# A two-layer relational graph attention kernel: the first keys are asked for after the query spread instead of beside it

## The chip, the cores and the metric

The kernel runs on one core of one Trainium2 chip. The metric is the device time of the whole program in microseconds (us). Work is divided among TensorE (PE), VectorE (DVE), ScalarE (ACT), GpSimd (POOL) and SyncE (SP), each with its own instruction stream; they meet at semaphores only. Sixteen DMA engines move data between DRAM and the on-chip memory.

## The reference

A graph of 1250 nodes (768 features) and 20000 edges, each with a source, a target and one of three types. A graph convolution comes first, then two relational attention layers (4 heads, then 1 head). Of one attention layer, what matters here:

```python
xr = jnp.einsum('nd,rdf->rnf', x, W)      # rows of the three relations
oi = xr[etype, dst]; oj = xr[etype, src]
qi = oi @ q                               # query score of the edge's target
kj = oj @ k                               # key score of the edge's source
alpha = leaky_relu(qi + kj, 0.2)
m = segment_max(alpha, dst)
e = exp(alpha - m[dst]); z = segment_sum(e, dst)
a = e / (z[dst] + 1e-16)
out = segment_sum(a * oj, dst) + b
```

## The kernel before, in words

Edges are sorted by target into slots of 128. Ten tiles of 128 nodes own the slots; two slots make a pair. The first node tile has far more pairs than the others, since low node numbers are drawn as targets more often. In this data there are 83 pairs.

Each attention layer `l` (1, 2) begins with the scores. Both scores of a node are computed first, per relation, without the big projection. Then two things are brought to the edge slots:

- **The query score, on TensorE.** `spread(j, q16, ...)` multiplies one-hot matrices (`stT`) with the ten tiles of query values. It is a loop for each tile, with six pairs in each turn: 12 slots, 36 small matmuls in layer 1 (line 1172) and 12 in layer 2 (line 1169). Over the ten tiles there are 17 turns, 612 or 204 matmuls. `spread_close` (line 1177) ends it and raises `q_spread[l]`.
- **The key score, on GpSimd.** `kst` is written to DRAM (line 396, `s_keys`), and `ask_keys(n)` asks for batch `n` by 12 indirect DMAs, each of 128 rows of 4 floats (line 490). An ask waits until the one 4 before it (layer 1) or 2 before it (layer 2) has landed. They go in GpSimd's own order.

VectorE waits for `q_spread[l]` (line 907), forms `qs` (lines 911 to 921) and raises `qs_ready`. GpSimd, once it has asked for batches 0 and 1 and `qs_ready` is there, does `score(0)` (lines 500, 504, 508: sum, the negative part, `al`), asks for batch 2, does `score(1)`, asks for batch 3, and so on for 14 batches. VectorE follows with the running maxima of the pairs whose `al` is there (lines 944, 959, 964), and at the end of a node tile with `maxima` (line 934).

On TensorE, after the query spread and once `spread_read` says that VectorE has read the banks, comes `project`: 30 node tiles (3 relations of 10) of 24 matmuls each (line 1255). `MAX_AT` puts between them the steps of the maxima: after project 11 the transposes of maxima of tile 0 (line 1273), after 14 of tile 1, after 17 of tile 2 and the spread of maxima of tile 0, and so on; the last ones stand after project 29. For a transpose TensorE waits for VectorE (`z_in`, `z_read`). After all of it GpSimd gathers the projected rows (line 459) for the weighted sums, which begin when TensorE gives the ring free (line 1283).

The maxima's spread uses the same function `spread` and the same lines 1172 and 1169.

SP loads the weights of the second relation in layer 1 (line 380) once VectorE has ended `prepare`, and those of the third relation during the projections.

Of the kernel before, what the change touches and what calls it, by code (L numbers as in the profile page):

```python
# [92 lines left out]
def gnn_kernel(nc, x, src, dst, edge_type, W0, b0, W1, q1, k1, b1, W2, q2, k2, b2, out):  # L93
# [12 lines left out]
    with ExitStack() as ctx:  # L106
# [3 lines left out]
        def sem(name):  # L110
            return ctx.enter_context(nc.semaphore(name))
# [173 lines left out]
        q_spread = {l: sem(f"q_spread{l}") for l in (1, 2)}  # L285
# [28 lines left out]
        def load_bounds(eng):  # L314

            eng.wait_ge(bounds_ready, 1)
            return [0] + [eng.value_load(bounds[0:1, j:j + 1], min_val=j if j < NT else (E + PAIR - 1) // PAIR, max_val=MAXPAIRS) for j in range(1, NT + 1)]
# [107 lines left out]
        @block.gpsimd  # L425
        def _(pool):
            nc.gpsimd.iota(iota_f[:, :], [[1, T]], base=0, channel_multiplier=0, allow_small_or_imprecise_dtypes=True).then_inc(pool_c, 1)
            nc.gpsimd.iota(iota_h[:, :], [[1, T]], base=0, channel_multiplier=0, allow_small_or_imprecise_dtypes=True).then_inc(pool_c, 1)
            nc.gpsimd.iota(iota_p[:, :], [[0, 1]], base=0, channel_multiplier=1, allow_small_or_imprecise_dtypes=True).then_inc(pool_c, 1)
            nc.gpsimd.memset(half[:, :], -0.5).then_inc(pool_c, 1)  # L430
            nc.gpsimd.memset(zero16[:, :], 0.0).then_inc(pool_c, 1)
            nc.gpsimd.memset(ones[:, :], 1.0).then_inc(pool_c, 1)
            nc.gpsimd.memset(idxr[:, T:T + KB], 0).then_inc(pool_c, 1)
            pool.wait_ge(pool_c, 7)
            bnd = load_bounds(pool)
            pool.wait_ge(slots_f, 1)
            pool.sem_inc(turn, 1)

            def targets(first, end):
                for c in range(first * PB, end * PB):  # L440

                    pool.wait_ge(perm_free, c + PB + 1)
                    pool.sem_inc(turn, 1)
                    nc.gpsimd.tensor_scalar(oh_tg[:, c % PB, :], iota_h[0:EP, 0:P], dloc[:, c:c + 1], None, ALU.is_equal).then_inc(tg_in, 1)  # L444

            targets(0, 1)
            pool.wait_ge(var_ready, 1)
            nc.gpsimd.tensor_tensor(rstd[:, :], vare[:, :], half[:, :], ALU.pow).then_inc(rstd_ready, 1)
            targets(1, GROUPS)
            pool.wait_ge(deg_ready, 1)  # L450
            nc.gpsimd.tensor_tensor(dinv[:, :], deg[:, :], half[:, :], ALU.pow).then_inc(dinv_ready, 1)
            groups = (bnd[NT] + (RING - 1)) // RING
            rest = (bnd[NT] + (RING - 1 - RING * FIXED)) // RING

            def gather_rows(l, idx):

                for t in range(2 * RING * FIXED):
                    pool.wait_ge(w_used[l], t + 1)
                    nc.gpsimd.indirect_dma_start(ring[:, t % (2 * RING), 0:WIDTH[l]], None, rows[l], bass.IndirectOffsetOnAxis(idx[:, t:t + 1], 0)).then_inc(g_sem[l][t % (2 * RING)], 16)  # L459

                with pool.Fori(0, rest) as g:
                    for side in range(2):

                        pool.wait_ge(g_in[l], 2 * RING * g + (2 * RING * FIXED + RING * side + 1))
                        nc.gpsimd.tensor_copy(idxs[:, RING * side:RING * (side + 1)], idx[:, ds(g * (2 * RING) + (2 * RING * FIXED + RING * side), RING)]).then_inc(ix[l], 1)
                        pool.wait_ge(ix[l], 2 * g + (side + 1))
                        pool.sem_inc(turn, 1)
                        for s in range(RING * side, RING * (side + 1)):
                            if s % 2 == 0:

                                pool.wait_ge(w_used[l], g * (2 * RING) + (2 * RING * FIXED + s + 2))
                                pool.sem_inc(turn, 1)
                            nc.gpsimd.indirect_dma_start(ring[:, s, 0:WIDTH[l]], None, rows[l], bass.IndirectOffsetOnAxis(idxs[:, s:s + 1], 0)).then_inc(g_sem[l][s], 16)

            pool.wait_ge(slots_ready, 1)
            pool.wait_ge(s_rows0, 16 * (NT + 1))
            gather_rows(0, idx0)
            pool.wait_ge(var_ready, 2)
            nc.gpsimd.tensor_tensor(rstd[:, :], vare[:, :], half[:, :], ALU.pow).then_inc(rstd_ready, 1)
            for l in (1, 2):  # L480
                H = HEADS[l]

                flight = KFLIGHT[l]

                def ask_keys(n):

                    for t in range(n * KB, (n + 1) * KB):
                        if t >= flight:
                            pool.wait_ge(k_in[l][t % flight], 16 * (t // flight))
                        nc.gpsimd.indirect_dma_start(kb[:, n % KSEMS, t % KB, 0:4], None, keys[l], bass.IndirectOffsetOnAxis(idxr[:, t:t + 1], 0)).then_inc(k_in[l][t % flight], 16)  # L490

                def score(n, slot, lows, looped=False):

                    batch = al[:, ds(n * (KB * H), KB * H)]
                    for s in range(flight):
                        pool.wait_ge(k_in[l][s], n * (16 * KB // flight) + 16 * KB // flight)
                    if looped or n > 0:
                        pool.wait_ge(al_step[l], n * (KB // 2))
                    pool.sem_inc(turn, 1)
                    nc.gpsimd.tensor_tensor(summed[:, 0:KB * H].rearrange("p (c h) -> p c h", h=H), kb[:, slot, :, 0:H], qs[:, ds(n * (KB * H), KB * H)].rearrange("p (c h) -> p c h", h=H), ALU.add).then_inc(k_sum[l], 1)  # L500
                    pool.wait_ge(k_sum[l], n + 1)
                    if looped:
                        pool.sem_inc(turn, 1)
                    nc.gpsimd.tensor_scalar(low[:, 0:KB * H], summed[:, 0:KB * H], 0.0, SLOPE - 1.0, ALU.min, ALU.mult).then_inc(k_low[l], 1)
                    pool.wait_ge(k_low[l], lows)
                    if looped:
                        pool.sem_inc(turn, 1)
                    nc.gpsimd.tensor_tensor(batch, summed[:, 0:KB * H], low[:, 0:KB * H], ALU.add).then_inc(al_step[l], KB // 2)  # L508

                pool.wait_ge(g_in[l - 1], 2 * RING * groups + (RING + 1))  # L510
                pool.sem_inc(turn, 1)
                pool.wait_ge(s_keys, 16 * R * l)
                ask_keys(0)
                ask_keys(1)
                pool.wait_ge(qs_ready, l)
                for n in range(KSURE):
                    score(n, n % KSEMS, n + 1)
                    if n + 2 < KSURE:
                        ask_keys(n + 2)


                with pool.Fori(1, (bnd[NT] + (255 - (KSURE + 1) * (KB // 2))) // 256 + 2) as m:
                    n = m + (KSURE - 1)
                    nc.gpsimd.tensor_copy(idxk[:, :], idxr[:, ds(n * KB, KB)]).then_inc(k_low[l], 1)
                    pool.wait_ge(k_low[l], m * 2 + (KSURE - 1))
                    pool.sem_inc(turn, 1)
                    for k in range(KB):
                        pool.wait_ge(k_in[l][k % flight], n * (16 * KB // flight) + 16 * (k // flight))
                        pool.sem_inc(turn, 1)
                        nc.gpsimd.indirect_dma_start(kb[:, KSURE % KSEMS, k, 0:4], None, keys[l], bass.IndirectOffsetOnAxis(idxk[:, k:k + 1], 0)).then_inc(k_in[l][k % flight], 16)  # L530
                    score(n, KSURE % KSEMS, m * 2 + KSURE, True)
                for side in range(2):
                    pool.wait_ge(stage_out[l][side], 16 * R * NT // 2)
                pool.wait_ge(rows_go[l], 1)
                gather_rows(l, idxr)
# [791 lines left out]
```

## Time and profile before

| | |
|---|---|
| median of 3 runs | 1750.67 us (1749.24 to 1755.21) |
| the profiled execution's own time | 1749.11 us |
| its span | 1747.3 us |
| PE busy | 1504.7 us (86%), 6326 matmuls |
| POOL busy | 1019.1 us (58%) |
| DVE busy | 927.5 us (53%) |
| ACT busy | 220.0 us (13%) |
| POOL line 490 (asks for keys) | 312 of them, 331.3 us busy |

Busy time is a sum over stages that have different limits. What the change meets is read from the stages where it stands: in layer 1 from about 485 us to 865 us, in layer 2 from about 1155 us to 1482 us.

### The profile page before, as it was taken

Reading aid. Unit: us, or ns where it says so; the run is one execution under the profiler, and the core shown is the slowest. Engines: PE = TensorE matmul, PEld = TensorE weight load, DVE = VectorE, ACT = ScalarE, POOL = GpSimd, SP = SyncE. Lnnn points to the kernel's source line nnn. Section 1 sums busy time; section 2 is a strip of 40 time slices with the busy share of each in tenths; the row PEclk is TensorE's granted clock in tenths of the full one; section 3 lists DMA queues with packets and bytes.
Section 4 is the critical chain, followed back from the end, with each engine's and each line's share of the span. In section 5 each row is a group of like instructions: output and inputs, shape, how many; then the busy total and the mean of one; then the engine's idle time right before and its main releaser. Section 6 shows DMA issues by size and latency. Waiting matters only on the chain.

```text
span 1747.3 us, 25349 instructions
## 1 busy us (share of the span) xinstructions
PE 1504.7 (86%) x6326; PEld 879.1 (50%) x6330; DVE 927.5 (53%) x2169; ACT 220.0 (13%) x530; POOL 1019.1 (58%) x1112
## 2 busy tenths in 40 slices
PE   5989999889955998699799989955997998898986
PEld 2445554555544554466554445433554655454553
DVE  8576722333342888888677777603433345222232
ACT  1545200000000111011100023320110111000000
POOL 1598266664433778873167777515656662666664
PEclk9988999999975999789899999965998999999999
DMA  8201588888720222111288887630231111888888
GB/s 299 103 19 41 189 266 267 267 290 264 240 66 2 56 89 59 20 38 38 84 264 264 262 252 243 195 105 2 55 110 38 38 47 54 276 263 265 263 259 269
DMA packets 86808, 271.76 MB, mean 156 GB/s; under 512 B 32156, under 2 KB 32531, under 8 KB 86743
## 3 DMA queue, kind: packets, MB, share of 16 engines
q0 software_dynamic: 51072, 199.44, 37.8%
q1 hardware_dynamic: 34807, 65.62, 10.5%
q10 hardware_dynamic: 864, 5.90, 0.9%
q8 instruction: 34, 0.56, 0.1%
q14 instruction: 31, 0.25, 0.0%
HBM read 239.28 MB, written 31.62 MB: 155 GB/s over the span
## 4 chain that ended last, share of the span: by engine, by line
PE 67%; issue 12%; POOL 9%; DMA 6%; DVE 4%; ACT 1%; DVEq 1%; another core or an unknown queue 0%; POOLq 0%; SPq 0%; PEldq 0%; ACTq 0%
PE ps L1255 13%; PE ps L1295 12%; PE ps L1228 11%; POOL ring L490 6%; PE ps L1297 6%; PE ps L1298 6%; PE ps L1126 5%; DMA ring<-keys,idxr 4%; PE ps L1172 3%; PE ps L1169 2%; PE ps L1189 2%; PE ps L1076 2%; PE ps L1047 1%; PE ps L1089 1%; DMA ring<-rows,idxr 1%
## 5 line engine op out<-in xcount | busy, mean ns | idle before, releaser
L1255 PE MATMUL ps<-wreg,hT 128*128 128x384 f32 x1440 | 488.4, 502 | 7.3 <-PEq L1248 6.7
L490 POOL DMA_INDIRECT ring<-keys,idxr x312 | 331.3, 1062 | 193.6 <-issue 80.1
L459 POOL DMA_INDIRECT ring<-rows,idxr x304 | 311.1, 1024 | 220.8 <-PEq L1283 76.3
L1255 PEld LDWEIGHTS ps<-wreg,hT 128*128 128x128 f32 x1440 | 281.3, 197 | 203.1 <-issue 25.9
L1295 PE MATMUL ps<-ring,zw 128*128 x664 | 230.5, 500 | 26.1 <-DVE zw L1024 17.0
L1228 PE MATMUL ps<-ring,zw 128*128 x664 | 226.0, 497 | 24.0 <-DVE zw L853 12.5
L959 DVE TENSOR_TENSOR hn<-hn,al 128x1024 f32 (+1 forms) x166 | 137.5, 828 | 169.2 <-POOL al L508 107.5
L459 POOL DMA_INDIRECT ring<-rows,idx x152 | 145.9, 960 | 118.3 <-PE ps L1228 65.4
L1295 PEld LDWEIGHTS ps<-ring,zw 128*128 128x128 f32 x664 | 124.0, 192 | 126.5 <-issue 57.0
L1228 PEld LDWEIGHTS ps<-ring,zw 128*128 128x128 f32 x664 | 124.6, 192 | 119.9 <-issue 54.6
L1022 DVE TENSOR_TENSOR ring<-ring,al x166 | 159.3, 960 | 39.8 <-SPq L377 21.1
L1297 PE MATMUL ps<-ring,zw 128*128 x332 | 138.7, 500 | 29.8 <-DVE zw L1027 25.0
L1027 DVE TENSOR_SCALAR zw<-iota_f,tl,al 128x128 f32<-128x128 f32 x166 | 60.3, 368 | 181.8 <-PE ps L1298 116.1
L853 DVE TENSOR_SCALAR zw<-iota_f,tl,ring 128x128 f32<-128x128 f32 x166 | 58.4, 356 | 180.6 <-PE ps L1228 129.2
L444 POOL TENSOR_SCALAR stT<-iota_h,stT 125x128 f16<-125x128 f16 x160 | 106.5, 683 | 56.6 <-PE ps L1091 28.6
L964 DVE TENSOR_TENSOR zw<-zw,hn 128x1024 f32<-128x1024 f32 (+1 forms) x166 | 136.3, 821 | 0.1
L1298 PE MATMUL ps<-ring,zw 128*128 x332 | 135.2, 489 | 0.0
L1297 PEld LDWEIGHTS ps<-ring,zw 128*128 128x128 f32 x332 | 60.5, 191 | 81.5 <-issue 49.0
L1126 PE MATMUL ps<-ring,hT 128*128 128x384 f32 x240 | 88.0, 523 | 0.0
L1298 PEld LDWEIGHTS ps<-ring,zw 128*128 128x128 f32 x332 | 63.4, 191 | 44.3 <-issue 0.6
L944 DVE TENSOR_SCALAR hn<-iota_f,tl 128x128 f32 x332 | 82.4, 296 | 0.3 <-issue 0.3
L638 ACT ACTIVATE stage<-ps,rstd 128x384 f32<-128x384 f32 x60 | 34.9, 582 | 328.4 <-PE ps L1255 267.0
(185 smaller groups left out, 1231.4 us busy)
## 6 DMA issues: line engine op xcount, KB each, us to landing
wreg<-in_L_gnn_W SPq DMA_DIRECT2D x11, 2304.0 KB, 9.2
rows<-stage SPq DMA_DIRECT2D x30, 386.0 KB
rows<-stage SPq DMA_DIRECT2D x30, 384.5 KB
stT<-targets_row ACTq DMA_DIRECT2D x6, 960.0 KB
ring<-keys,idxr POOLq DMA_INDIRECT x312
ring<-rows,idxr POOLq DMA_INDIRECT x304
rows<-stT SPq DMA_DIRECT2D x10, 384.0 KB, 3.0
xs<-in_x SPq DMA_DIRECT2D x3, 1152.0 KB, 13.3
```

The lines of the kernel that those rows point to most:

```text
L444: nc.gpsimd.tensor_scalar(oh_tg[:, c % PB, :], iota_h[0:EP, 0:P], dloc[:, c:c + 1], None, ALU.is_equal).then_inc(tg_in, 1)
L459: nc.gpsimd.indirect_dma_start(ring[:, t % (2 * RING), 0:WIDTH[l]], None, rows[l], bass.IndirectOffsetOnAxis(idx[:, t:t + 1], 0)).then_inc ...
L490: nc.gpsimd.indirect_dma_start(kb[:, n % KSEMS, t % KB, 0:4], None, keys[l], bass.IndirectOffsetOnAxis(idxr[:, t:t + 1], 0)).then_inc(k_in ...
L959: V.tensor_tensor(scored[:, :, 0:H, :], negm[:, ds(i % 2, 1), :, :].rearrange("p a b c -> p (a b) c").unsqueeze(2).to_broadcast([P, 2, H, P]),
L964: V.tensor_tensor(run, run, scored[:, :, 0:H, :], ALU.max).then_inc(m_chain[l], 1)
L1022: V.tensor_tensor(row, row, al[:, ds(t * H, H)].unsqueeze(2).to_broadcast([P, H, ROW // H]), ALU.mult).then_inc(rows_scaled, 1)
L1126: last = mm(ps[:, 4 - 2 * (nt % 2) + h, 0:HALF], hT[:, k, nt * P:(nt + 1) * P], w0s[:, k, h * HALF:(h + 1) * HALF], start=(k == 0), stop=( ...
L1228: last = mm(ps[:, 2 * (j % 2) + a, 0:HALF], zw[:, 0, b, 0, :], ring[:, ds((i % RING) * 2 + b, 1), a * HALF:(a + 1) * HALF].rearrange("p o ...
L1255: last = mm(ps[:, 2 * (nt % 2) + h, 0:HALF], hT[:, k, nt * P:(nt + 1) * P], wreg[:, r % 2, k, h * HALF:(h + 1) * HALF], start=(k == 0), st ...
L1295: last = mm(ps[:, 2 * (j % 2) + a, 0:2 * W], zw[:, 0, b, 0, :], row[:, a * 2 * W:(a + 1) * 2 * W], start=False, stop=False, skip_group_che ...
L1297: mm(ps[:, 2 * (j % 2), 0:HALF], zw[:, 0, b, 0, :], row[:, 0:HALF], start=False, stop=False, skip_group_check=True)
L1298: last = mm(ps[:, 2 * (j % 2) + 1, 0:HALF + 1], zw[:, 0, b, 0, :], row[:, HALF:D + 1], start=False, stop=False, skip_group_check=True)
```

## The change

```diff
                 pool.wait_ge(s_keys, 16 * R * l)
+
+                pool.wait_ge(q_spread[l], 1)
                 ask_keys(0)
                 ask_keys(1)
                 pool.wait_ge(qs_ready, l)
```

GpSimd gets one wait more in each layer: before its first ask for keys it waits until TensorE has closed the spread of the query values. No instruction is added, removed or reordered on any engine; the order within GpSimd's stream is that of before. The first rows of GpSimd's stream that differ stand at the start of layer 1, `rstd` being the last thing computed before it:

```order
 L479 TENSOR_TENSOR rstd<-vare,half 128x10 [waits var_ready]
 L510 ISA
-L490 DMA ring<-keys,idxr 128x4 [waits g_in0,s_keys]
+L490 DMA ring<-keys,idxr 128x4 [waits g_in0,q_spread1,s_keys]
 L490 DMA ring<-keys,idxr 128x4 x3
 L490 DMA ring<-keys,idxr 128x4 [waits k_in1_0]
```

Only the first of the 24 asks has the new wait (`q_spread1`); the other 23 and `score(0)` stand behind it. In layer 2 the same row waits for `q_spread2`.

## Rows read from the trace of the kernel before

**Rows 1.** Timeline, layer 1, spread and asks: start, length, engine, line [idle before <- releaser]
```profile
498.96 1.55 PE L1172 MATMUL ps<-q,stT 128*128 128x12 bf16 x36 [0.23 <-issue]
503.48 1.05 POOL L490 DMA_INDIRECT ring<-keys,idxr  x1 [13.88 <-DMA keys<-kst]
507.24 0.38 SPq L380 DMA_DIRECT2D wreg<-in_L_gnn_W  x1
...
534.42 0.94 POOL L490 DMA_INDIRECT ring<-keys,idxr  x1 [0.30 <-issue]
...
553.98 3.11 DVE L914 TENSOR_TENSOR ring<-ps,rmask 128x192 f32<-128x192 f32 x12 [44.98 <-PE ps L1177]
...
560.10 0.28 POOL L500 TENSOR_TENSOR summed<-ring,etmp 128x48 f32<-128x48 f32 x1 [24.73 <-DVEq L923]
```

**Rows 2.** Line 1172 from 507.4 to 539.2 us: count, shortest/median/longest ns, first and last start
```profile
L1172 PE MATMUL ps<-q,stT x144: 167/173/192, 507.5 to 538.8; 128*128 128x12 bf16 x144
```

**Rows 3.** Line 1172 from 539 to 553.6 us, the same columns
```profile
L1172 PE MATMUL ps<-q,stT x289: 171/173/193, 538.8 to 553.5; 128*128 128x12 bf16 x145
```

**Rows 4.** Timeline, layer 2, spread and asks
```profile
1164.84 1.53 PE L1169 MATMUL ps<-q,stT 128*128 128x9 bf16 x12 [0.25 <-issue]
1166.71 1.50 PE L1169 MATMUL ps<-q,stT 128*128 128x9 bf16 x12 [0.33 <-issue]
...
1171.64 0.94 POOL L490 DMA_INDIRECT ring<-keys,idxr  x1 [42.12 <-DMA keys<-kst]
...
1203.09 0.94 POOL L490 DMA_INDIRECT ring<-keys,idxr  x1 [0.30 <-issue]
...
1208.71 0.18 PE L1177 MATMUL ps<-zero 128*128 128x8 bf16 x1
...
1213.31 8.81 DVE L928 TENSOR_TENSOR xs<-xs,bias 128x768 f32<-128x768 f32 x10
1213.43 0.91 POOL L500 TENSOR_TENSOR summed<-ring,etmp 128x12 f32<-128x12 f32 x1 [9.40 <-DVEq L923]
1216.25 1.57 POOL L490 DMA_INDIRECT ring<-keys,idxr  x1 [0.16 <-issue]
1223.24 0.94 POOL L490 DMA_INDIRECT ring<-keys,idxr  x1 [0.30 <-issue]
1236.80 0.23 POOL L500 TENSOR_TENSOR summed<-ring,etmp 128x12 f32<-128x12 f32 x1
```

**Rows 5.** Line 1169 from 1187 to 1207 us, as in Rows 2
```profile
L1169 PE MATMUL ps<-q,stT x39: 168/187/189, 1186.8 to 1206.6; 128*128 128x9 bf16 x39
```

**Rows 6.** Waits from 553 to 870 us: engine, line <- releaser: total, times, longest
```profile
DVE hn L959 <- POOL al L508: 9.8, 8, 1.5
```

**Rows 7.** Timeline, TensorE, layer 1: where it waits for the maxima
```profile
685.76 1.94 PE L1273 MATMUL ps<-ident,zw 128*128 128x128 f32 x8 [7.74 <-DVE mx L934]
713.70 1.06 PE L1273 MATMUL ps<-ident,zw 128*128 128x128 f32 x8 [1.75 <-DVE mx L934]
```

**Rows 8.** Waits from 1208 to 1490 us
```profile
DVE hn L959 <- POOL al L508: 97.8, 11, 15.9
POOL ring L459 <- PEq L1283: 19.9, 1, 19.9
```

**Rows 9.** Timeline, TensorE, layer 2
```profile
1340.02 0.66 PE L1273 MATMUL ps<-ident,zw 128*128 128x128 f32 x2 [9.39 <-DVE mx L934]
...
1366.17 0.92 PE L1169 MATMUL ps<-m,stT 128*128 128x3 bf16 x24
1372.74 17.21 PE L1255 MATMUL ps<-wreg,hT 128*128 128x384 f32 x48
```

**Rows 10.** Timeline, GpSimd, layer 2: one of the later batches of asks
```profile
1336.77 0.22 POOL L500 TENSOR_TENSOR summed<-ring,etmp 128x12 f32<-128x12 f32 x1
1338.12 1.04 POOL L490 DMA_INDIRECT ring<-keys,idxr  x1 [0.43 <-issue]
...
1355.76 0.22 POOL L500 TENSOR_TENSOR summed<-ring,etmp 128x12 f32<-128x12 f32 x1
```

**Rows 11.** Line 1172 from 714 to 737.2 us, as in Rows 2
```profile
L1172 PE MATMUL ps<-m,stT x178: 163/166/186, 714.6 to 737.2; 128*128 128x4 bf16 x178
```

## The prediction

> **What bounds the kernel now.** I read four views: the timeline over both score stages, the instructions of the spread's line by stretches, the waits of each layer's projections, and TensorE's timeline through them.
>
> Layer 1, score stage. The spread of queries starts its second turn at 498.96 us; VectorE, which waits for its end, goes on at 553.98, after 45 us idle [rows 1]. In 539 to 553.6 us TensorE does 288 matmuls (289 less the one that starts at 538.8), so 8 turns in 14.4 us or 1.80 us a turn [rows 3]. In 507.4 to 539.2 it does 144, so 4 turns in 31.8 us or 7.9 a turn, though one matmul takes the same median 173 ns in both [rows 2, 3]. The asks for keys run from 503.48 to 535.4 [rows 1]: the slow stretch lies beside them, the fast one behind. Layer 2 shows it again: turns 1.87 us apart at 1164.84, before the asks, and 39 matmuls, some three turns of 12, in the 20 us from 1187 [rows 4, 5]; the asks end at 1204.0 and the spread closes at 1208.7 [rows 4]. What the slow stretches share is asks in flight, and both end some 3 us after the last ask is through on GpSimd.
>
> GpSimd meanwhile is done early: it has asked for both batches by 535.4 and waits 24.7 us for `qs_ready`, until 560.10 [rows 1]; in layer 2 it waits 9.4 us, until 1213.43 [rows 4]. So before, the first score hangs on the spread, and the 24 asks lie free beside it.
>
> Projections. VectorE waits for `al` by 1.5 us a batch in layer 1, eight times [rows 6], and TensorE waits for VectorE's maxima twice, until 685.76 and 713.70 [rows 7]. In layer 2 VectorE waits 97.8 us in all for `al` [rows 8]: GpSimd's asks set the pace there, up to 1340.02, where TensorE waits 9.39 us for the maxima [rows 9]. From then on TensorE is the bound. So what decides is when the scores come, not when TensorE starts to project.
>
> **The change, part by part.** Nothing is added or removed but two waits. I price them against the profiled execution, 1749.1 us (span 1747.3 and 1.8 around it); the median is 1.6 above that.
>
> *The spread gets faster.* Of 17 turns, 16 are left at 498.96. At 1.84 us (between 1.80 in rows 3 and 1.87 in rows 4) they take 29.4, so the close would be at 528.4 + 0.2 = 528.6. One thing stays beside it: the weight load issued at 507.24 [rows 1], whose share in the slow turns the trace doesn't separate. Bounds for it are 0 and 5 us; I take 1.4, nearer to nothing since layer 2 has no such load in its slow stretch. That makes 530.0, 23.9 earlier than 553.9. In layer 2: 1164.84 + 16 x 1.84 + 0.2 = 1194.5, 14.4 earlier than 1208.9.
>
> *The 24 asks go behind it.* This is the cost. All that stands behind the waiting ask on GpSimd is 23 more asks and `score(0)`, and VectorE's whole chain of maxima waits for that.
> Layer 1: before they took 503.48 to 535.4, 31.9 us [rows 1]. The least that rows show is 0.94 busy and 0.30 between, 1.24 each, 30 us. A few will lie beside VectorE's `qs` work and cost more; I take 31.3, and 0.2 for the semaphore. Score(0) is then at 561.5, where before it was at 560.10: **+1.4 us**. The early close only pays the asks back. Bounds: 528.6 + 0.2 + 30.0 = 558.8, so -1.3; 533.6 + 0.2 + 31.9 = 565.7, so +5.6. VectorE's next wait for `al` carries this on [rows 6].
> Layer 2: the asks start at 1194.8. Beside VectorE's bias addition four asks took 7.0 us, 1.75 each (1216.25 to 1223.24 [rows 4]); VectorE's work there, from the close to the end of that addition, is 1208.9 to 1222.1 or 13 us [rows 4], room for 8 such asks. In a later batch 12 took 1338.12 to 1355.76 less 0.2, so 1.45 each [rows 10]. That makes 8 x 1.75 + 16 x 1.45 = 37.2, and score(0) at 1232.0. It takes 1.35 to the next ask [rows 10], batch 2's asks 17.4, and score(1) stands at 1250.8. Before it stood at 1236.80 [rows 4]: **+14.0 us**. (Score(0) alone is 18.6 later; 4.6 comes back since batch 2 no longer lies beside the bias addition.) Bounds for the 24: 30 us as above, which gives +6.8; and the pace of before's batch 2, 1216.25 to 1236.80, 1.71 each, 41 us, which gives +17.8.
>
> *TensorE starts earlier.* By 23.9 and 14.4 us, and this I cost at nothing: the cover is its waits for the maxima. At 685.76 and 713.70 it had to wait already [rows 7], so the lead is spent there; what follows keeps its distances. In layer 2 it waits 9.39 at 1340.02 [rows 9]; it will wait 9.4 + 14.4 + 14 = some 38 us over the steps up to that point, then run the same 140 us. Nothing of GpSimd's slack behind (19.9 us before line 459 [rows 8]) helps, as the delay enters before TensorE's last wait.
>
> *The sum:* 1.4 + 14.0 = 15.4, so 1749.1 + 15.4 = 1764.5 us. With the bounds: 5.5 to 23.4, so 1754.6 to 1772.5.
>
> **A rule weighed.** An ask moves 16 bytes a row, and yet turns stretch from 1.80 to 7.9 us beside them [rows 2, 3]. The Trainium skill, SBUF — State Buffer, section "SBUF: two separate sides", says the reverse: a DMA can't slow a compute operation, and TensorE never waits for anyone at the memory. By that rule moving the asks leaves the spread as slow as it was. The trace speaks against it as far as coincidence can, twice over, and what is slow is the time between matmuls, not the matmul. It is the first rival below.
>
> **Rivals.**
> *R1, the asks don't slow the spread.* The slow stretches would be TensorE's own, at a fixed place in its stream. Then it closes at 553.9 and 1208.9, and the asks come wholly on top. Layer 1: 553.9 + 0.2 + 31.3 = 585.4, +25.3. Layer 2: 1208.9 + 0.3 + 37.2 + 1.4 + 17.4 = 1265.2, +28.4. Time 1802.8. For it: the slow part doesn't begin with the first ask (layer 2: 1171.6 against some 1187). Against: it ends with the last ask in both layers. Chance 7%.
> *R2, TensorE is the bound of the projections.* This is the one on the faster side. Then the leads count in full and the late scores are hidden: 1749.1 - 23.9 - 14.4 = 1710.8. For it: 86% busy, and no wait for the maxima after 713.70 and 1340.02. Against: those waits themselves. It decides the other way only if the 48 asks take 15.4 us less than I say, 53 in place of 68.5, or 1.1 us each; no row is under 1.24. Chance 3%.
> *R3, layer 2 absorbs the delay.* GpSimd has 19.9 us of slack at the end [rows 8]; if TensorE's steps could wait on it without loss, only layer 1's +1.4 stays: 1750.5. Against: TensorE's wait until 1340.02, with half of the 30 projections still ahead. Chance 4%.
> *R4, a slow stretch appears elsewhere.* The spread of maxima of tile 0 runs beside asks in both layers. Layer 1's needed 22.6 us for five turns (178 matmuls) [rows 11], layer 2's 6.6 for its five (1366.17 to 1372.74) [rows 9]. If the shifted phase makes layer 2's as slow relative to 1.84 a turn, 13 us come on top where TensorE is the bound: 1777.5. Against: only the phase changes. Chance 8%.
>
> **How the numbers follow.** The forecast has 78%, with its own range 1755 to 1773. R4 lies above, R1 far above, R2 and R3 below. I leave R1, R2 and R3 out and take in R4: 1755 to 1778. A measurement of this kernel tells about 0.3% (5.3 us) from no change. Faster: R2 and next to nothing of the forecast, 0.03. Same: R3 and the low edge of the forecast (5.5 to 6), 0.05. Slower: 0.92.
>
> **What would show it.** In the changed profile: the query spread of layer 1 closes near 530 without a turn over 4 us (wrong: near 554, R1); the first ask right behind it; `score(0)` near 561.5, so layer 1 ends about where it did. In layer 2: the close near 1196, 24 asks of 1.5 us in the mean, score(1) near 1252; VectorE's wait for `al` over 97.8; TensorE's waits at line 1273, 9.5 in layer 1 and 9.4 in layer 2 before [rows 7, 9], near 9.5 + 23.9 + 1.4 = 35 and 38, and the one that ended at 1340.02 ends near 1355. If TensorE doesn't wait more there, the cover I gave the lead is missing and the sign is wrong. If the asks in layer 2 go at 1.25, the delay is half of what I say.

## The result, and the profile after

Over 18 runs each, before has a median of 1753.43 us and the changed kernel 1779.47 us. The ratio is 1.0121, 95% interval 1.0101 to 1.0141: slower by 18 to 25 us, where 15.4 was forecast. Put on the 1750.67 us from which the forecast started, the ratio gives 1771.9, within the forecast's 1755 to 1778. The ratio is taken over fast executions alone, which leaves out five of the changed kernel's 18 (1788 to 1801 us) and, in the experiments below, single ones of 3780 and 5587 us; over all 18 the medians lie 26 us apart. The profiled execution of the changed kernel has a span of 1771.2 us, 23.9 over before's.

First the spread and the asks in the changed kernel. The rows are its timeline (start, length, engine, line), layer 1 and then layer 2; they answer to [rows 1] and [rows 4].

```profile
525.10 1.55 PE L1174 MATMUL ps<-q,stT 128*128 128x12 bf16 x36 [0.21 <-issue]
526.70 0.18 PE L1179 MATMUL ps<-zero 128*128 128x8 bf16 x1
...
527.66 1.03 POOL L490 DMA_INDIRECT ring<-keys,idxr  x1 [40.92 <-PE ps L1179]
...
556.46 0.94 POOL L490 DMA_INDIRECT ring<-keys,idxr  x1 [0.30 <-issue]
557.42 0.30 POOL L500 TENSOR_TENSOR summed<-ring,etmp 128x48 f32<-128x48 f32 x1
...
1202.18 0.18 PE L1179 MATMUL ps<-zero 128*128 128x8 bf16 x1
...
1203.12 0.94 POOL L490 DMA_INDIRECT ring<-keys,idxr  x1 [65.22 <-PE ps L1179]
...
1240.06 0.23 POOL L500 TENSOR_TENSOR summed<-ring,etmp 128x12 f32<-128x12 f32 x1
...
1259.23 0.23 POOL L500 TENSOR_TENSOR summed<-ring,etmp 128x12 f32<-128x12 f32 x1
```

The asks start behind the close of the spread, and the spread has no slow turn left in this execution. Counted from its first matmul (the opening of the banks, 496.6 and 1163.0 us in before, 493.9 and 1171.3 after), it closes after 32.8 us in layer 1 (57.1 before) and 30.9 in layer 2 (45.7 before). `score(0)` of layer 1 stands 63.5 us after the opening in both kernels: the earlier close pays the asks back to the tenth. (From here on +63.5 means 63.5 us after the opening of that layer.) `score(1)` of layer 2 stands at +88.0, before +73.8.

But layer 1 didn't end where it did. TensorE's timeline in its first projections, which had no gap in before:

```profile
530.46 23.87 PE L1257 MATMUL ps<-wreg,hT 128*128 128x384 f32 x68 [3.58 <-PEq L1250]
554.54 0.48 PE L1257 MATMUL ps<-wreg,hT 128*128 128x384 f32 x1 [0.20 <-issue]
557.34 0.48 PE L1257 MATMUL ps<-wreg,hT 128*128 128x384 f32 x1 [2.32 <-issue]
560.13 0.80 PE L1257 MATMUL ps<-wreg,hT 128*128 128x384 f32 x1 [2.32 <-issue]
...
578.47 0.99 PE L1257 MATMUL ps<-wreg,hT 128*128 128x384 f32 x1 [0.62 <-issue]
```

A matmul of which one began every 0.35 us (68 in 23.87) now begins only every 2.1 to 2.8 us, for 24 us. TensorE's granted clock falls from 1.0 to 0.5 (2.4 to 1.2 GHz) at 557.8, with the engine mostly idle, and is 1.0 again from 588.5; the matmuls themselves get longer with it, as the view of line 1257 shows for 554 to 580 and for 590 to 640 us (count, shortest/median/longest ns, first and last start):

```profile
L1257 PE MATMUL ps<-wreg,hT x14: 482/799/994, 553.5 to 579.9; 128*128 128x384 f32 x14
...
L1257 PE MATMUL ps<-wreg,hT x154: 483/486/583, 590.0 to 640.0; 128*128 128x384 f32 x154
```

VectorE meets the same, in its maxima:

```profile
563.76 1.22 DVE L966 TENSOR_TENSOR zw<-zw,hn 128x1024 f32<-128x1024 f32 x1
570.73 1.22 DVE L961 TENSOR_TENSOR hn<-hn,al 128x1024 f32 x1 [5.75 <-issue]
573.56 0.50 DVE L946 TENSOR_SCALAR hn<-iota_f,tl 128x128 f32 x1 [1.61 <-issue]
...
580.82 1.23 DVE L961 TENSOR_TENSOR hn<-hn,al 128x1024 f32 x1 [3.85 <-issue]
```

What is slow is again the time between instructions ("issue"). The sequencers' own steps show it, in the view of one line's instructions (count, shortest/median/longest ns, first and last start). The first row is VectorE's in the changed kernel from 564 to 586 us, the second the same line after it, from 590 to 640:

```profile
L946 DVEq ALU_OP  x3: 4/40/712, 574.9 to 585.8; - x3
...
L946 DVEq ALU_OP  x16: 40/40/40, 591.9 to 638.0; - x16
```

and of before, TensorE's in the slow end of layer 2's spread, 1187 to 1207 us:

```profile
L1169 PEldq FUSED_REGOPS  x34: 2/18/702, 1187.0 to 1206.5; - x34
```

Register steps of 0.04 us and less take 0.7 us at times. In layer 1's slow spread in before the register steps keep their 0.037 us; there TensorE pauses between its instructions, by 0.7, 1.4, 2.1 or 2.8 us. They aren't spread evenly: the first of 0.7 comes at 506.4 us, 2.9 us after the first ask, they lie dense from 514.6 on, and one turn of 36 matmuls takes 21.8 us. So a slow stretch of layer 1 is gone from the spread, and another stands in the projections and VectorE's maxima.

There is a third, which the kernel before has too: the spread of the maxima of tile 0 in layer 1, 180 matmuls. The first row is before's in a later measurement, where nothing is slow, the second the changed kernel's here; they answer to [rows 11]:

```profile
L1172 PE MATMUL ps<-m,stT x179: 164/166/186, 669.1 to 677.3; 128*128 128x4 bf16 x179
...
L1174 PE MATMUL ps<-m,stT x180: 164/166/187, 718.4 to 737.4; 128*128 128x4 bf16 x180
```

It takes 8.2 us there, 22.7 in before's first trace and 19.0 in the changed kernel's. TensorE's waits for the maxima, which answer to [rows 7, 9]:

```profile
689.45 1.94 PE L1275 MATMUL ps<-ident,zw 128*128 128x128 f32 x8 [11.67 <-DVE mx L936]
717.48 1.07 PE L1275 MATMUL ps<-ident,zw 128*128 128x128 f32 x8 [1.34 <-DVE mx L936]
...
1325.36 0.69 PE L1275 MATMUL ps<-ident,zw 128*128 128x128 f32 x2 [24.22 <-DVEq L968]
1363.09 0.66 PE L1275 MATMUL ps<-ident,zw 128*128 128x128 f32 x2 [12.19 <-DVE mx L936]
```

In layer 2 they are 36.4 us together (38 forecast), in layer 1 only 13.0 (35 forecast), since TensorE's own slow stretch in the projections ate the lead there. The stages of the two first traces and of two later ones (both kernels in a later measurement on one chip, next section), from opening to the close of the maxima's spread for a layer:

| us | before | after | before, later | after, later |
|---|---|---|---|---|
| up to layer 1's opening | 496.6 | 493.9 | 475.4 | 476.0 |
| layer 1, scores and projections | 365.4 | 376.0 | 338.8 | 361.9 |
| between, weighted sums of layer 1 | 301.0 | 301.4 | 281.9 | 286.2 |
| layer 2, scores and projections | 317.1 | 331.5 | 305.8 | 330.7 |
| the rest | 267.2 | 268.5 | 244.3 | 243.9 |

### The profile page after: what moved, and what is told of

The parts are those of the page before. It is cut to its first block, busy times and chain, and to the rows that moved or that the text cites. A ratio compares the mean times of both kernels' runs of the same rounds, so it can differ in the third digit from the quotient of the medians.

```text
span 1771.2 us, 25351 instructions
## 1 busy us (share of the span) xinstructions
PE 1515.7 (86%) x6326; PEld 879.6 (50%) x6330; DVE 927.7 (52%) x2169; ACT 219.8 (12%) x530; POOL 1016.3 (57%) x1112
## 4 chain that ended last, share of the span: by engine, by line
PE 66%; issue 11%; DVE 8%; DMA 7%; POOL 4%; DVEq 2%; ACT 1%; another core or an unknown queue 0%; SPq 0%; POOLq 0%; PEldq 0%; ACTq 0%
PE ps L1257 13%; PE ps L1297 13%; PE ps L1230 11%; PE ps L1299 6%; PE ps L1300 6%; PE ps L1128 5%; DMA ring<-keys,idxr 5%; DVE zw L966 3%; PE ps L1174 3%; POOL ring L490 3%; PE ps L1171 2%; PE ps L1191 2%; PE ps L1078 2%; PE ps L1049 2%; PE ps L1091 1%
## 5 line engine op out<-in xcount | busy, mean ns | idle before, releaser
L1257 PE MATMUL ps<-wreg,hT 128*128 128x384 f32 x1440 | 500.9, 509 | 27.2 <-issue 20.0
L490 POOL DMA_INDIRECT ring<-keys,idxr x312 | 327.2, 1049 | 243.5 <-PE ps L1179 106.1
L444 POOL TENSOR_SCALAR stT<-iota_h,stT 125x128 f16<-125x128 f16 x160 | 106.4, 683 | 57.9 <-PE ps L1093 29.8
```

The costliest lines, as they stand in the source:

```text
L1257: last = mm(ps[:, 2 * (nt % 2) + h, 0:HALF], hT[:, k, nt * P:(nt + 1) * P], wreg[:, r % 2, k, h * HALF:(h + 1) * HALF], start=(k == 0), st ...
```

## The experiments

The later measurements ran on two chips, the two called padded (480 and 280) and four asks in flight (first time) on one, number 7, and all others on the other, number 15. Both ran before at 1647 to 1649 us in place of 1753. The record has no number for the chip of the first measurement, so that it was a third chip, and not another condition of one of these two, isn't shown; I write "first measurement" for it. Every ratio is to before in the same measurement. The stages of the two runs on chip 7 are set against before's trace on chip 15; what the edit doesn't touch agrees there (layer 1 of the kernel with four asks in flight 338.1 us, before 338.8).

**One layer at a time.** The new line under `if l == 1:`, or under `if l == 2:`:

```diff
+                if l == 1:
+                    pool.wait_ge(q_spread[l], 1)
                 ask_keys(0)
```

Expected of layer 1 alone: 

> The new wait in layer 1 alone; layer 2 as before. Theory A (the asks for keys slow the other engines' sequencers wherever they lie; in layer 1 the slow stretch was only moved from the spread into the projections and VectorE's maxima): 6 to 11 us slower than before, and a stretch of some 20 us in the profile, after 545 us, in which matmuls of line 1255 are 2 us or more apart. Theory B (that stretch was a chance of one execution, layer 1 costs only the asks' later start): 0 to 2 us slower, projections without a gap.

Measured: 1669.87 us against 1646.58, ratio 1.0138 (1.011 to 1.0166), 23 us slower. There is no gap in the projections; both theories fail on the size.

Expected of layer 2 alone: 

> The new wait in layer 2 alone. Both theories: 14 us slower than before (24 asks at 1.5 us on the path less the 14 us that the spread gets faster, less 5 us that batch 2 wins from not lying beside the bias addition); score(1) 14 us later after the start of the spread than before. If layer 2's share were hidden or larger: 0, or over 20.

Measured: 1666.05 us, ratio 1.0127 (1.0097 to 1.0157), 21 us slower, above the 14 expected. The reason for both is in layer 1 of this kernel, which is before's: with 24 asks beside it, the spread isn't slow in this trace. TensorE and GpSimd in that stretch:

```profile
487.17 1.55 PE L1174 MATMUL ps<-q,stT 128*128 128x12 bf16 x36 [0.27 <-issue]
488.95 1.68 PE L1174 MATMUL ps<-q,stT 128*128 128x12 bf16 x36 [0.22 <-issue]
...
507.27 0.18 PE L1179 MATMUL ps<-zero 128*128 128x8 bf16 x1
...
512.17 0.94 POOL L490 DMA_INDIRECT ring<-keys,idxr  x1 [0.30 <-issue]
513.42 0.94 POOL L490 DMA_INDIRECT ring<-keys,idxr  x1 [0.30 <-issue]
514.38 0.30 POOL L500 TENSOR_TENSOR summed<-ring,etmp 128x48 f32<-128x48 f32 x1
```

It closes 32.7 us after opening and `score(0)` stands at +39.8, ready by the asks; with the wait, in layer 1 alone, it stands at +63.9. The wait costs the asks in full where the spread loses nothing to them.

**Half of the asks behind.** `ask_keys(0)`, then the wait, then `ask_keys(1)`:

```diff
                 ask_keys(0)
+                pool.wait_ge(q_spread[l], 1)
                 ask_keys(1)
```

Expected: 

> Batch 0 is asked for beside the spread as before, batch 1 only when the spread is closed; both layers. If 12 asks are too few to slow the spread much: it closes after some 38 us in layer 1 (31 without asks, 57 with 24) and 32 us in layer 2, batch 1 costs 15 us in layer 1 and 19 in layer 2, so score(0) is some 8 us earlier than before in layer 1, and score(1) some 4 us earlier in layer 2: 5 to 12 us faster than before in all. If even 12 asks slow the spread by as much as 24 did: layer 1 15 us slower, layer 2 some 15 slower, 30 in all.

Measured: 1659.24 us, ratio 1.0077 (1.0053 to 1.01), 13 us slower. Neither branch of the expectation came: the spread closes at +33.2 with the 12 asks beside it, and `score(0)` comes at +48.3, 8.5 later than 39.8. With fewer asks behind the close, less is lost. It was run once more with the next pair. Expected: 

> Batch 0 asked for beside the spread, batch 1 behind it, once more. Theory C: on a chip without slow stretches 12 to 14 us slower than before, as in its first run; on one with them 0 to 12 us faster than before, since 12 asks leave most of the spread free. Rival: 12 to 14 us slower everywhere.

Measured: 1663.56 against 1647.85, ratio 1.0094 (1.007 to 1.0118). The answer is the same; what it does where slow stretches occur was not seen.

**Plain DMAs in place of the gathers.** In before's order; the first two batches of keys are then not the edges' own, so this kernel leaves the right scores out:

```diff
+                        if n < 2:
+                            pool.dma_start(kb[:, n % KSEMS, t % KB, 0:4], keys[l][t * P:(t + 1) * P, :]).then_inc(k_in[l][t % flight], 16)
+                            continue
                         nc.gpsimd.indirect_dma_start(kb[:, n % KSEMS, t % KB, 0:4], ...
```

Expected: 

> Before's order, but batches 0 and 1 (24 asks a layer) are plain DMAs from GpSimd's queue of 128 consecutive rows of the key table in place of gathers by an index (the scores of these batches are not those of the reference). If what slows the spread is the many small descriptors that GpSimd writes: slow turns of 4 us and more stay, the spread of layer 1 takes over 45 us. If it is the reading of the index or the scattered rows of the gather: the spread takes some 32 us.

It ran once, in 1639.58 us, and the spread took 33.0 us. As gathers don't slow the spread on this chip either, it doesn't decide its question.

**Both kernels on one chip.** Expected of the changed kernel: 

> The changed kernel once more, both layers. The runs of one layer each showed spreads that asks don't slow at all (layer 1 closes 32.7 us after it opens with the asks beside it, where the first trace had 57.1), and before itself at 1647 in place of 1753 us. Theory C (the slow stretches belong to the chip, not to the program): where before runs at some 1647 us, both shares add up, 23 + 20, so 40 to 46 us slower; where before runs near 1750, some 21 to 26 slower, as first measured. Rival (one and the same mechanism everywhere, which the two single changes happened to miss): 21 to 26 slower wherever it runs.

Expected of before: 

> The kernel before, for its trace beside that of the changed one on the same chip. Theory C: with a time near 1647, the spread of layer 1 closes 33 us after it opens although 24 asks lie beside it; with a time near 1750, after 50 us or more. Rival: after 50 us or more at either time.

Measured: the changed kernel 1696.68 against 1647.85, ratio 1.0293 (1.0266 to 1.0319), 48 us slower; before 1647.99 in its profiled execution, with the spread of layer 1 closed after 32.8 us. That is theory C's forecast, the change a little dearer than I said; that the chip is what makes the stretches isn't shown by it. The waits of TensorE for the maxima in layer 1, of before (its trace from this chip) and then of the changed kernel. The spread closes at +32.8 and +32.5, so TensorE has no lead here; the waits grow because the scores come 23.7 us later (`score(0)` at +63.2 against +39.5):

```profile
640.30 1.09 PE L1273 MATMUL ps<-ident,zw 128*128 128x128 f32 x4 [9.07 <-DVE mx L934]
```

```profile
626.26 1.97 PE L1275 MATMUL ps<-ident,zw 128*128 128x128 f32 x8 [18.02 <-DVEq L968]
...
664.31 1.94 PE L1275 MATMUL ps<-ident,zw 128*128 128x128 f32 x8 [11.99 <-DVE mx L936]
```

The two traces are 52.4 us apart (1698.6 and 1646.2 us of span), and the table above splits that: 23.1 in layer 1, 24.9 in layer 2, 4.3 between and nothing else of note. These are close to what R1 priced, 25.3 and 28.4: where the spread isn't slow, the asks come wholly on top.

What the slow stretches cost in the first measurement can only be bounded by the difference between the two pairs of columns, as everything else that differs is in it: 26.6 and 11.3 us in the two layers of before, 14.1 and 0.8 in the changed kernel. In layer 1 of before `score(0)` comes 24.0 us later (+63.5 against +39.5) and the maxima's spread of tile 0 takes 14.5 us more (22.7 against 8.2), while TensorE's later waits of 8.6 and 3.2 us for the maxima fall away. Read so, the change saves 12.5 + 10.5 = 23.0 us of slow stretches and costs 23.1 + 24.9 = 48.0. That the 25.0 left equals the two first traces' 10.6 + 14.4 is no test: it follows from how the 23.0 was formed. The next experiment is the test.

**A spread made long by hand.** If that is so, then before, with its spread as long as in the first trace but by other means, must lose most of its lead over the changed kernel.

```diff
+                for _ in range(pad):
+                    mm(psf[:, c:c + 8], zero16[:, 0:P], zero16[:, 0:8], start=True, stop=True)
                 mm(psf[:, c:c + 8], ...).then_inc(done, 1)
```

Expected with 480 and 280: 

> Before's order, with 480 (layer 1) and 280 (layer 2) idle matmuls of 8 columns ahead of the close of the query spread, to make it as long as it was in the first traces: 57 us after its opening in layer 1 and 45 in layer 2, where this chip's traces have 33 and 31. Theory C (what the change costs on a chip is the 24 asks less what its spread loses to them): at 0.05 us a matmul layer 1 is 24 us slower than before, layer 2 some 4, together 26 to 30 us; the changed kernel, 49 us slower than before on this chip, then stands 19 to 23 us over this one, as it stood 21 to 26 over before in the first measurement. Rival (the length of the spread isn't what differed): padded costs under 10 us or over 45.

Measured: 1667.43 against 1649.02, ratio 1.0115 (1.0087 to 1.0143). An idle matmul took 0.027 to 0.030 us and not 0.05, so the spread closed at +46.5 and +38.2; `score(0)` of layer 1 moved 13.4 us and the end of the layer 13.4. Expected with 870 and 520: 

> As the padded kernel, with 870 and 520 idle matmuls, since one took only 0.028 us and the spreads were lengthened by 13.7 and 7.4 us. Theory C: the spread of layer 1 now closes near 57 us, score(0) near 63.5 and the layer ends 24 us later than before; layer 2 closes near 45 with score(0) at 49 to 50, 4 later; together 26 to 32 us slower than before. The changed kernel on the same kind of chip is 49 slower, so 17 to 23 more. Rival: well under 20 us slower.

Measured: 1684.52 against 1646.82, ratio 1.0232 (1.0213 to 1.025), 38 us slower. The spreads close at +58.0 and +46.2, `score(0)` of layer 1 at +64.4, and that layer is 24.9 us longer, as expected. Layer 2 is 13.9 longer and not 4: its `score(1)` is at +73.0 where before has +63.8 in its later trace, so there I mis-sized what a later `qs` costs. The changed kernel is 10 us over this one (1.0293 to 1.0232), below the 17 to 23 expected. In the first measurement it stood 18 to 25 over before, which these 10 and the 14.1 us of its own slow stretches in layer 1 account for. So it is borne out that a spread as long as in the first trace takes 38 of the 48 us by which the change loses, whatever made it long.

**Four asks in flight in layer 2.**

```diff
-KFLIGHT = {1: 4, 2: 2}
+KFLIGHT = {1: 4, 2: 4}
```

Expected: 

> Before's order, with four asks in flight in layer 2 in place of two. If the asks' pace sets layer 2 up to TensorE's last wait for the maxima (as the sum took it): GpSimd's waits for landed keys in layer 2 (48 us in all before) go, an ask takes 1.3 in place of 1.5 us, score(1) comes some 5 us earlier, TensorE's last wait is gone and the kernel is 8 to 14 us faster; no more, since TensorE has only that much to win (its waits of 13.7 us in layer 2). If it was TensorE all along: no change.

Measured: 1630.08 against 1649.02, ratio 0.988 (0.9849 to 0.9912). The waits of layer 2, of before (its later trace) and then of this kernel:

```profile
DVE hn L959 <- POOL al L508: 122.3, 14, 15.3
POOL ring L490 <- DMA ring<-keys,idxr: 65.1, 92, 5.0
POOL ring L459 <- PEq L1283: 18.7, 1, 18.7
PE ps L1273 <- DVE mx L934: 13.7, 1, 13.7
```

```profile
DVE hn L959 <- POOL al L508: 71.3, 12, 9.7
POOL ring L490 <- issue: 43.9, 140, 0.5
POOL ring L459 <- PEq L1283: 42.4, 1, 42.4
```

GpSimd's waits for landed keys fall from 65.1 to 5.6 us, and TensorE's wait for the maxima is gone. The gain, some 20 us, is more than TensorE's 13.7. Layer 2 is 17.8 shorter (288.0 for 305.8; 288.3 in the repeat on chip 15). Of the 4.1 us beyond the wait, 1.7 lie in the 72 projections right behind it: from first to last start they took 24.6 us in before, where the granted clock was 0.5 for 13.7 us up to +170.2, and 22.9 here, where it was 1.0. Another 2.3 lie in one spread of maxima (24 matmuls at +250.8 in 3.0 us against 0.7); why isn't known.

It was repeated beside the changed kernel with the same line. Expected of the repeat: 

> Before's order with four asks in flight in layer 2, beside the other two on one chip: again 16 to 24 us faster than before.

Measured: 1630.02 against 1646.82, ratio 0.9895 (0.9875 to 0.9914). Expected of the changed kernel with it: 

> The changed kernel with four asks in flight in layer 2. Layer 1's price stays, 23 us. In layer 2 the asks (1.3 us each) no longer set the pace up to the end of the projections: GpSimd is 42 us ahead there with four in flight, and TensorE waits nowhere. Theory: of the 20 to 25 us by which the scores of layer 2 come later, TensorE's lead of none and its free steps absorb part: it now waits for the maxima of tile 0 and 1 for 8 to 15 us; the kernel is 31 to 38 us slower than before's order with four in flight. Rival (the delay of the scores always reaches the end in full): 44 to 50 us slower than that.

Measured: 1670.8, ratio to before 1.0148 (1.0129 to 1.0167), so 41 us over before's order with four in flight: between the two expectations. Layer 1 is 23.7 longer. In layer 2 `score(1)` is 23.8 later (+81.0, +57.2) and the layer 17.2 longer (305.5, 288.3): TensorE's free steps absorb 6.6, less than I said, and it waits 6.7 and 6.3 us for the maxima.

Before's order with four in flight is the best version, 1.1 to 1.2% under before and 4% under the changed kernel on chip 15.

## Why the prediction was right, and where not

*The spread gets faster.* Right in the first measurement, in size too: the closes came 32.8 and 30.9 us after opening, where I had 33.4 (530.0 less 496.6) and 31.5. The 1.4 us for the weight load was not needed. My 7.9 us a turn was a mean over unlike turns: 76 of the 144 matmuls are through by 514 us, and the other 68 take the 25 us behind. Rival R1, a slow part at a fixed place in TensorE's stream, is out for this pair of traces; with one trace of each kernel it isn't excluded that such stretches also come and go by themselves. On chip 15 there was nothing to win.

*The 24 asks go behind it.* Right. Layer 2: 24 asks took from 1203.12 to 1240.06, 36.9 us, where I had 37.2; `score(1)` came 14.2 later, where I had 14.0; the layer grew by 14.4. Layer 1: `score(0)` was unchanged in place of 1.4 later; the 24 asks took 29.8 us, their lower bound, because VectorE had nothing to do beside most of them.

*Layer 1 ends about where it did.* This step failed: +10.6 and not +1.4. I had priced slow stretches as bound to the query spread, and R4 named a new one for layer 2's maxima only, whose spread of tile 0 stayed at 6.3 us. A new one came in layer 1, 27 us after the first ask, in the projections and in VectorE's maxima, where before had none: VectorE's seventh pass of line 961 begins 12.5 us later after the opening than before's, and TensorE's second wait for the maxima ends 6.5 us later (+223.6 against +217.1). The spread of tile 0 then wins 3.7 of that back (19.0 us against 22.7), and up to +312.7 (before +301.6) TensorE falls behind to 11.1, with pauses in the spreads of tiles 1 and 2 (4.5 and 5.7 us against 2.9 and 2.6) and in the projections between. So the whole came out above the forecast by layer 1: layer 2 cost 14.4 us (14.0 forecast), layer 1 10.6 (1.4 forecast).

That one execution had these stretches there is shown; that most runs have them isn't, as there is one trace of the changed kernel from the first measurement. Its 18 times spread over 1761 to 1801 us, before's over 1746 to 1763, which would fit a cost that falls differently from run to run.

*TensorE's lead costs and gains nothing.* Right in layer 2 (36.4 us of waits, 38 forecast). In layer 1 it waited 13.0 us and not 35, as the slow projections had used up the rest; the wait at 717.48 still hangs on VectorE, so the lead gained nothing there either. R2 and R3 are out: no lead reached the end, and layer 2 absorbed nothing.

*What was luck.* The sign and the size in layer 2 follow from the asks as priced. That the measurement came near 20 and not near 50 rests on slow turns in before's spread which the forecast took as given; on chip 15 the same change costs 48 us, far outside the range, with the asks priced equally well.

*The rule weighed.* The Trainium skill, SBUF — State Buffer, section "SBUF: two separate sides", has a DMA never slow a compute operation. On chip 15 the runs agree (32.8 us with the asks beside the spread, 32.5 without). In the first measurement the spread took 57.1 us with them and 32.8 without. The matmuls in it kept their median of 173 ns, and the time went into pauses between instructions and register steps of 0.7 us, so the rule, which is on the memory, isn't refuted by it; it only doesn't cover what was lost.

Open stays what makes the stretches. In both traces that have steps of 0.7 us, asks or gathers are in flight beside every one of them, but their place isn't that of the asks: pauses of 0.7 us begin 2.9 us after the first ask in layer 1 of before, 5.5 in its layer 2 and 27 in layer 1 of the changed kernel, and beside layer 2's asks in the changed kernel there are none. The packets of one of the queues that bring instructions (q8, 16 KB each) took as long in either case, 0.9 to 2.0 us in before's first trace and 0.9 to 2.3 in its later one. No experiment ran where the stretches occur.

## What to carry to other kernels

A transfer that runs free beside other work is dear once it is put on the path: count every issue behind the new wait (24 x 1.25 to 1.5 us here), and set against it only what the trace shows the other work to lose. When a trace shows such a loss as gaps between instructions with no releaser, measure a second time, on another chip if there is one, before reordering for it: here some 23 of 48 us came back in one measurement and nothing in the other. Looking at the queue that waits for a landing with two in flight was worth more (20 us) than either order.

## What the hardware showed that I had not expected

- The same kernel took 1753 us in the first measurement and 1647 to 1649 us on two chips later. The profiled spans differ by 101.1 us, 37.9 of it in the two score and projection stages and 63 in the rest, of which 42 us lie in the weighted sums and the end (301.0 + 267.2 against 281.9 + 244.3), where GpSimd gathers rows.
- In slow stretches single register steps of a sequencer take 0.70 to 0.71 us and not 0.04, on TensorE's weight loads, VectorE and a few times SyncE, and pauses between TensorE's instructions are 0.7 us or multiples of it. In the 12 later traces no register step lasts over 0.26 us. VectorE's operations keep their lengths; TensorE's projections took 0.80 us in place of 0.49 while the granted clock was 0.5.
- An idle bf16 matmul of 8 columns with fixed addresses came every 0.027 to 0.030 us; one of the spread, 12 columns with an address from a register for each three, every 0.05.
